# Attention with four maxima banks and three score banks: the second head pair shares one bank

## The reference

```python
# layer 0, attention: mask applied after the softmax (keys at or behind the query)
p = softmax(einsum('bhqd,bhkd->bhqk', q, k) / sqrt(s));  p = p * triu(ones)
# layer 0, feed-forward: causal mask before the softmax, heads of 8 dimensions
probs = softmax(where(causal, scores, finfo.min))
# layer 1, attention: causal mask before the softmax
weights = softmax(score - NEG * (1.0 - causal))
z = einsum('bhqk,bhkd->bhqd', probs, v)
```

## Time and profile before

| | |
|---|---|
| median of 3 runs | 2807.44 us (2797.06 to 2808.77) |
| the profiled execution | 2814.0 us, its span 2812.3 us |
| att0, first exponential to last z | 139.6 to 849 us |
| att1 | 992 to 1426 us |
| att2 | 1734 to 2168 us |
| busy over the span | PE 86%, DVE 70%, ACT 51%, POOL 13% |

### The profile page before, as it was taken

One profiled execution on the slowest core, in us unless ns is written; L12 is line 12 of the kernel. 1 busy time (PEld: TensorE's weight loads), 2 busy tenths in 40 slices (PEclk: granted clock), 3 DMA queues, 4 the chain that ended last, 5 costly groups with the idle time before them and its releaser, 6 DMA issues. The chain is left out here.

```text
span 2812.3 us, 40150 instructions
## 1 busy us (share of the span) xinstructions
PE 2408.5 (86%) x14416; PEld 1101.5 (39%) x14416; DVE 1976.6 (70%) x3999; ACT 1428.3 (51%) x2105; POOL 379.6 (13%) x559
## 2 busy tenths in 40 slices
PE   4799999999984499999959976999998789888997
PEld 2333333333322243333324433433333346534663
DVE  4789889888944588888735546888883765458553
ACT  1067677766772036777622221466775346533662
POOL 2000000000000100001100001000012243214330
PEclk8599999999997669999969985899997889988998
DMA  4300100000000510212200015012122333124320
GB/s 177 60 14 12 21 12 6 12 8 11 4 3 1 131 29 6 42 26 43 48 4 0 0 37 117 6 26 41 27 41 33 113 131 118 57 68 152 112 88 15
DMA packets 86068, 130.23 MB, mean 46 GB/s; under 512 B 28560, under 2 KB 50704, under 8 KB 83856
## 3 DMA queue, kind: packets, MB, share of 16 engines
q1 hardware_dynamic: 82592, 117.49, 16.9%
q10 hardware_dynamic: 3312, 10.59, 1.3%
HBM read 59.16 MB, written 13.63 MB: 26 GB/s over the span
## 5 line engine op out<-in xcount | busy, mean ns | idle before, releaser
L700 ACT ACTIVATE att_probs<-psum 128x1024 f32<-128x1024 f32 (+3 forms) x1152 | 1037.8, 951 | 628.9 <-PE psum L748 627.4
L658 DVE TENSOR_REDUCE att_part_max<-psum 128x1 f32<-128x512 f32 x1792 | 1128.1, 684 | 168.2 <-PE psum L730 164.3
L730 PE MATMUL psum<-k_rows,att_q_rows 64*128 64x512 f32 (+3 forms) x2304 | 822.7, 487 | 102.0 <-DMA att_q_rows<-q_pieces 55.3
L730 PEld LDWEIGHTS psum<-k_rows,att_q_rows 64*128 64x128 f32 x2304 | 363.1, 198 | 761.2 <-DVE att_part_max L658 535.2
L773 PE MATMUL psum<-att_probs,v_aug 128*9 128x512 f32 (+3 forms) x3712 | 450.4, 560 | 18.9 <-ACT att_z_sb L692 18.8
L748 PE MATMUL psum<-att_q_rows,k_rows 64*128 64x512 f32 (+3 forms) x2304 | 423.4, 409 | 14.0 <-ACT att_probs L700 9.7
L655 DVE CUSTOM_DVE_ANT_0 att_masked<-psum,mask_max_sb 128x384 bf16<-128x384 f32 (+3 forms) x512 | 232.9, 486 | 83.9 <-PE psum L730 79.1
L748 PEld LDWEIGHTS psum<-att_q_rows,k_rows 64*128 64x128 f32 x2304 | 242.5, 196 | 90.6 <-ACT att_probs L700 57.9
L608 POOL TENSOR_SCALAR_AFFINE_SELECT att_probs<-att_probs 128x256 f32<-128x256 f32 x256 | 102.5, 406 | 822.0 <-ACT att_probs L700 819.6
L1392 ACT ACTIVATE latt_probs<-psum,latt_bias,latt_scale 128x192 f32<-128x192 f32 x256 | 127.3, 507 | 120.3 <-DVE latt_bias L1431 120.3
L769 PE MATMUL psum<-att_probs,att_one_only 128*9 128x512 f32 (+3 forms) x1280 | 147.9, 534 | 10.7 <-ACT att_z_sb L692 10.5
(11 more groups left out here) (259 smaller groups left out, 2453.6 us busy)
## 6 DMA issues: line engine op xcount, KB each, us to landing
k_rows<-k_pieces SPq DMA_DIRECT2D x96, 256.0 KB, 8.0
lproj_swapped<-lproj_other SPq DMA_DIRECT2D x128, 128.0 KB, 2.1
latt_k<-local_k_T SPq DMA_DIRECT2D x32, 384.0 KB, 3.0
att_q_rows<-q_pieces SPq DMA_DIRECT2D x168, 64.0 KB
lproj_table<-in_tables SPq DMA_DIRECT2D x16, 512.0 KB, 4.2
latt_q<-local_q_T SPq DMA_DIRECT2D x32, 256.0 KB, 2.4
latt_v_own<-local_v_tok SPq DMA_DIRECT2D x32, 256.0 KB, 2.3
k_pieces<-proj_piece SPq DMA_DIRECT2D x24, 256.0 KB, 2.5
```

Of the source, the lines that this page charges most:

```text
L658: nc.vector.tensor_reduce(column, ring[e % NRING][:, 0:w], AX.X, ALU.max).then_inc(ring_free, 1)
L700: nc.scalar.activation(probs[s % NPROBS][:, pr, :, at:BANK], st[pr][:, :, at:BANK], ACT.Exp, scale=scale).then_inc(st_free, 1)
L730: nc.tensor.matmul(ring[e % NRING][:, 0:w], q_rows[u % NQ][rows, pr, qt * P:(qt + 1) * P].bitcast(F32R), k_rows[b][rows, pr, kc * BANK:kc ...
```

## The change

The ring of maxima tiles gets a fourth bank, and the scores keep three: pair 0 has banks 0 and 1 as before, and both heads of pair 1 share bank 2, one after the other. A step is now: head 0 of pair 1, then heads 1 and 0 of pair 0 (`first_scores`, which wait for all three exponentials of the step before), then all of the step's maxima tiles, then head 1 of pair 1 (`last_scores`, which waits for the exponential of head 0 of that pair), then the products of step s - 2. ACT makes three exponentials in a step: 512, 1024 and 512 columns. `take_z` stands behind the second. SP's and POOL's waits count three exponentials in a step.

```diff
-NRING = 3
+NRING = 4
...
-        st = [bank(psum, 2 * pr, 2).rearrange("p (i q) -> p i q", i=2) for pr in range(2)]
-        ring = [bank(psum, 4 + b) for b in range(NRING)]
+        st = [bank(psum, 0, 2).rearrange("p (i q) -> p i q", i=2), bank(psum, 2)]
+        ring = [bank(psum, 3 + b) for b in range(NRING)]
...
-                    sp.wait_ge(st_full, 2 * plan.first_step[u + 1])
+                    sp.wait_ge(st_full, 3 * plan.first_step[u + 1])
...
-                        pool.wait_ge(st_free, 2 * s + pr + 1)
+                        pool.wait_ge(st_free, 3 * s + pr + 2)
...
-                for pr in range(2):
-                    act.wait_ge(st_full, 2 * s + pr + 1)
-                    nc.scalar.activation(probs[s % NPROBS][:, pr, :, at:BANK], st[pr][:, :, at:BANK], ACT.Exp, scale=scale).then_inc(st_free, 1)
-                    if pr == 0 and u > 0 and kb == 2:
-                        take_z(u - 1)
+                act.wait_ge(st_full, 3 * s + 1)
+                nc.scalar.activation(probs[s % NPROBS][:, 1, 0, at:BANK], st[1][:, at:BANK], ACT.Exp, scale=scale).then_inc(st_free, 1)
+                act.wait_ge(st_full, 3 * s + 2)
+                nc.scalar.activation(probs[s % NPROBS][:, 0, :, at:BANK], st[0][:, :, at:BANK], ACT.Exp, scale=scale).then_inc(st_free, 1)
+                if u > 0 and kb == 2:
+                    take_z(u - 1)
+                act.wait_ge(st_full, 3 * s + 3)
+                nc.scalar.activation(probs[s % NPROBS][:, 1, 1, at:BANK], st[1][:, at:BANK], ACT.Exp, scale=scale).then_inc(st_free, 1)
...
-            def scores(s, pr):
+            def score(s, pr, i, to):
                 u, kb = steps[s]
                 b = plan.k_load_of[u] % NK
                 at = plan.from_column(u, kb)
-                if s > 0:
-                    pe.wait_ge(st_free, 2 * (s - 1) + pr + 1)
-                for i in range(2):
-                    rows = slice(64 * i, 64 * i + ROWS)
-                    m = nc.tensor.matmul(st[pr][:, i, at:BANK], k_rows[b][rows, pr, kb * P:(kb + 1) * P].bitcast(F32R),
-                                         q_rows[u % NQ][rows, pr, at:BANK].bitcast(F32R), start=True, stop=True, skip_group_check=True)
-                m.then_inc(st_full, 1)
+                rows = slice(64 * i, 64 * i + ROWS)
+                return nc.tensor.matmul(to[:, at:BANK], k_rows[b][rows, pr, kb * P:(kb + 1) * P].bitcast(F32R),
+                                        q_rows[u % NQ][rows, pr, at:BANK].bitcast(F32R), start=True, stop=True, skip_group_check=True)
+
+            def first_scores(s):
+                if s > 0:
+                    pe.wait_ge(st_free, 3 * s)
+                score(s, 1, 0, st[1]).then_inc(st_full, 1)
+                score(s, 0, 1, st[0][:, 1, :])
+                score(s, 0, 0, st[0][:, 0, :]).then_inc(st_full, 1)
+
+            def last_scores(s):
+                pe.wait_ge(st_free, 3 * s + 1)
+                score(s, 1, 1, st[1]).then_inc(st_full, 1)
...
-                pe.wait_ge(st_free, 2 * s + 2)
+                pe.wait_ge(st_free, 3 * s + 3)
...
-                scores(s, 0)
-                scores(s, 1)
-                maxima(plan.issued_by(u, (kb + 0.5) / plan.blocks[u]))
+                first_scores(s)
+                maxima(plan.issued_by(u, (kb + 1) / plan.blocks[u]))
+                last_scores(s)
                 if s >= 2:
                     products(s - 2)
-                maxima(plan.issued_by(u, (kb + 1) / plan.blocks[u]))
```

## The result

| | before | after |
|---|---|---|
| median | 2805.67 us | 2917.21 us |
| runs | 4 (2797.06 to 2808.77) | 4 (2912.27 to 2920.83) |
| ratio, 95% interval | | 1.0398 (1.0372 to 1.0424) |
| span of the profiled execution | 2812.3 us | 2919.1 us |

The change makes the kernel 4.0% slower. The forecast was slower by 64 us; it is 107 between the profiled executions, and the median of 2917 lies 21 us above the forecast's upper end of 2896 (7 above 2910, the end of the wider range that was to hold 8 in 10).

A forecast was written before the change was run, and what follows sets the result against it. It took PE and DVE, bounding each other through three ring banks, to set the pace. Att0's +14 and two causal attentions at +25 gave +64 us: 2878 profiled, 2872 for a median, range 2845 to 2896.

The forecast's parts named there:

- What bounds the kernel before: Attentions: PE and DVE bound each other through three ring banks, 2.67 us a plain step; ACT is slack.
- ACT's circle: Changed step: first scores wait for all three exponentials of the step before, making 2.66 us whatever PE and DVE do.
- PE's circle: Changed step: last score waits for the first exponential, then products and the way to the next scores: 2.65 us.
- the diagonal step: Step of att0 with a diagonal product on top: 0.23 us more, 2.88 (before 2.91).
- the z step: Step in which z is copied: the copy stands behind two exponentials and products follow it, 3.63 us.
- five tiles: Step in att0's full units whose fifth tile waits for the first tile's reduction: about 3.2 us.
- The fourth bank does what it says, and wins nothing: Plain steps: DVE's wait is gone, but ACT is late next, so the gain is 0.01 us a step.
- The sum: Three attentions, added stage by stage against the windows before: att0 +14, each causal attention +25, together +64 us.
- the term for the clock: Thin steps, att0's last unit: at the half clock 3.9 us a step, 16 steps +20; if it stays up, 0.
- The clock falls in the thin steps: Rival: the clock falls in steps with few tiles, or latencies add up: 2896 to 2920 us; chance 0.14.
- The other rivals: Weight loads don't overlap, 2975, 0.01; cheaper, 2821 to 2845, 0.10; no change, 0.04; faster, about 2775, 0.04.
- weight loads do overlap: Rival claimed they don't within one row half: slots 0.41, steps 3.04, +165 over 430 full steps, 2975 us; chance 0.01.

The follow-up runs named there:

- the two ring experiments: Changed kernel with three ring banks instead of four: 3248.92 us; kernel before with all maxima tiles of a step ahead of its products: 3024.34 us.

## Why the prediction was wrong in size

- **What bounds the kernel before**: not tested by itself, but the reading (PE and DVE in a circle through three banks) agrees with the two ring experiments, whose steps the same terms gave as 3.1 and 3.3 to 3.4 for 3.14 and 3.38. One reading was wrong: a step of att0's last unit does not take 36.6 / 16 = 2.3. Its plain steps take 1.84 and 2.16 in turns, 2.0 in the mean; the 36.6 us hold three long first steps and the end. The sum went by the window, so it is not touched, but the change stretched these steps by a third, not by a sixth.
- **ACT's circle, 2.66; PE's, 2.65; the diagonal step, 2.88; the z step, 3.63; five tiles, 3.2**: measured 2.65, 2.65, 2.87, 3.62, 3.15. Halving the first exponential shortened the step and halving the third did not; so PE's circle with the wait for the first exponential is enough to hold 2.65. That ACT's is just as long follows from its terms in the timeline, and is not shown apart.
- **The fourth bank does what it says, and wins nothing**: right.
- **The sum**: att0's full units 0 (measured 630.4 for 629.4 us; the first, which starts at the half clock, is 2.4 longer, the others 1.4 shorter together), unit 14 48 (48.2), the start of a causal attention +5 (+5.9 in att1). Too small: att0's last unit +9, measured 56.0 for 37.5 up to the copy of z, +18.5; 16-step units +11, measured +15.7 in att1; 12-step +6, measured +11.0; 8-step +3.5, measured +9.1; 4-step 0, measured +4.8.
- **The step that failed** is the term for the clock. "If the clock stays up, 0" went into the sum. Its price, worked out as 3.9 us a step and up to 20 us, stood for att0's last unit alone and led only to a rival with a chance of 0.14. Measured, a half-clock step there takes 4.09, and seven long ones cost 10 us. What I did not price at all are the causal units, where 13 of 20 z-copy steps took 4.4 to 4.77 us for the 3.63 of the sum, and the steps behind them up to 4.1 for 2.66. The z-copy step already took 4.4 to 4.6 us in six places before the change, and I read only the mean clock of those windows, 0.98 and 0.94. A stretch in which the clock already falls now and then, and in which the change leaves PE waiting longer, should have had its price in the sum: 43 us were missing, and all but ten of them came in the causal attentions.
- The rival "The clock falls in the thin steps" gave 2896 to 2920 and is what happened; why the clock falls in one unit and not in the next is open. The other rivals were rightly small; weight loads do overlap in the new order, since the slots are 0.23 there too. The price of that rival was also added up short: 165 us of longer steps come on top of the +64 of the thin ones, about 3035 and not 2975.

## What to carry to other kernels

Draw the circle of a step for each shared buffer, with every latency in it: here two uses of one bank in a step, each waiting for its reader, made a floor of 2.65 us under every step, and a bank given to another ring couldn't pay for that, since the full steps took 2.67 anyway and the thin ones less. Before pricing a stretched step as time alone, look what the granted clock does in the stretches where PE already waits, in single steps and not in the mean over units. When an experiment repairs something in the changed kernel, make the same repair in the kernel before: only the pair shows whether the change broke it. And a small operation that others wait for, here the copy of z, belongs into its engine's idle time at the head of the step; that move alone made the kernel before 1.5% faster.

## What the runs showed that I had not expected

- A few idle matmuls can shorten a stage: four more in each step of att0's last unit, and it went from 56.0 to 47.5 us (clock 0.74 to 0.97). The same trick in the tiles ahead of the first step did nothing (0.50 both times).
- The same steps at either level: 2.65 and 4.09 us. How long the low level lasts is not the same from run to run: seven, five and all of att0's last steps in three kernels that differ there by the place of one copy or by one shorter exponential, and all of them again in the kernel with three ring banks, which has no tiles in that unit. Differences of 10 us between single executions are within that.
